# The value projection behind the output projection, and a feed-forward norm on transposed tokens

## The chip, the cores and the metric

The kernel runs on one core of a Trainium2 chip, in one launch. The metric is the time of the slowest core, here the only one, in microseconds of device time; lower is better. The engines are TensorE (PE, matmuls; PEld are its weight loads), VectorE (DVE), ScalarE (ACT), GpSimd (POOL) and SyncE (SP, which only issues transfers). Each has its own instruction queue and runs it in order. They wait for each other through semaphores.

## What is computed

The input is one sequence of 2048 tokens of 128 channels. A time-mixing layer comes first, then six layers of windowed attention and feed forward, then a layer norm. The change touches only the six layers (and takes one constant out of the first part). Cut to what matters:

```
for i in range(6):
    x = attn_layer(shift_tokens(x), Wqkv[i], ...) + x
    x = ffn_layer(shift_tokens(x), g[i], b[i], W1[i], b1[i], W2[i], b2[i]) + x

attn_layer:                              # 16 heads of 64, windows of 32 tokens
    q, k, v = split(x @ Wqkv)
    q, k = l2norm(q) * q_scale, l2norm(k) * k_scale
    q = q * cos * scale + rotate_half(q) * sin * scale      # and k, with 1 / scale
    out = softmax(8 * q @ k.T in the window and the one before) @ v
    return out @ Wo

ffn_layer:
    mu  = mean(x);  var = mean((x - mu) ** 2)               # over the 128 channels of a token
    xn  = (x - mu) / sqrt(var + 1e-5) * g + bln
    a, gate = split(xn @ W1 + b1)
    return a * gelu(gate) @ W2 + b2
```

`shift_tokens` takes the second half of the channels from the token before.

## The kernel before

The 2048 tokens are 16 tiles of 128, so the six layers are 96 tile steps, numbered s. The residual stream lies with channels on partitions, in `xa` (into attention) and `xb` (into feed forward). The work is a software pipeline, written out by hand: in step s the engines project tile p = s + 1 (q, k and v, and the norm and rotation of q and k), score tile a = s and weigh and sum tile b = s - 1. The feed forward works on two tiles at a time. In an odd step it makes the norm of a pair (`norm`) and narrows the pair before (`down`); in an even step it scales and widens (`up`). So two steps, an odd and an even one, are one period, and 48 such pairs make up the layers. A loop of 44 rounds holds most of them; the first and last steps are written out.

What sets the order is the source text alone: each engine has a `step` function, and its instructions go into that engine's queue as they stand there. No scheduler moves anything.

The banks in PSUM are shared. `bank_a` (`proj_a`) holds q, then v. `bank_b` (`proj_b`) holds k, then the narrowed product (second half, read into `xa`) and the norm's sums (first half), then two of the three widened chunks. `bank_s` (`att`) holds transposed probabilities, PV, the transposed heads and WO's product; `bank_t` (`turn`) the transposed q and k and the scores.

The lines that the steps below touch, with names as the profile gives them:
- TensorE: L1247 all transposes, L1280 projection of q, L1295 of k, L1306 PV, L1340 scores, L1352 projection of v, L1359 narrowing, L1364 centring (`centre` = identity less 1/128), L1371 spreading the deviations (`ones` times a diagonal), L1377 WO, L1383 variance, L1264 widening.
- VectorE: L1151 `sums` of squares, L88 to L104 an inverse root, L1176 `unit` (q, then k, divided by its norm), L1165 and L1168 `row_max` and `logits`, L1214 `norm_n`, L1219 `xa`, L1223 `xb`, L1228 `var_f`, L1234 `along` of k, L1183 `mass`.
- GpSimd: L1017 `turns`, L1025 and L1026 `shift_f`, L988 and L989 `shift_a`, L999 `across` of q, then of k, L1032 `along` of q, L1006 `rotated` of q, then of k, L1040 `rstd_f`.
- ScalarE: L1054 `squares`, L1083 and L1089 `q_t` and `k_t`, L1098 `rstd_diag`, L1104 `o_t`, L1113 the copy of v (`val`), L1061 `probs` (Exp), L1121 `normed`, L1128 and L1130 `dev` and `dev_sq`, L1068 gelu.
- SP: L945 and L948 spread a tile's v into windows, 16 transfers a step, once the copy of v is there.

Three waits matter around the change. The projection of q writes `bank_a`, so it waits for the copy of v (`v_laid`). The projection of k in an even step writes `bank_b`, so it waits for `var_kept` and for `xa_ready`, which VectorE raises when `xa` is done. And turning k waits for GpSimd's second `rotated`:

```python
pe.wait_ge(k_in, (layer_of(p) + 1) * 16)
after(pe, united[1], p)
if odd:
    after(pe, gated, NC_ * (h + 1))
else:
    if live["up"]:
        pe.wait_ge(var_kept, h + 2)
    after(pe, xa_ready, XA_BASE + h + 1 if not isinstance(h, int) or h >= 0 else 0)
```

Of the kernel before, what the change touches and what calls it, by code (L numbers as in the profile page):

```python
# [26 lines left out]
ALU = mybir.AluOpType  # L27
# [98 lines left out]
def build(nc, x, vectors, mix_w1, mix_w2, decay_w1, decay_w2, r_weights, r_norm, wqkv, wo, ffn, qk_scales,  # L126
          positions, carry, ident, band, level_masks, out):
    with ExitStack() as ctx:
# [15 lines left out]
        averager = sb("averager", [128, 128])  # L144
# [49 lines left out]
def time_mix(nc, ctx, given):  # L194
# [4 lines left out]
    xa, xb, x_tok, identity, identity_bf, band_f, band_bf, averager, ones, minus_half = (  # L199
        given[k] for k in ("xa", "xb", "x_tok", "identity", "identity_bf", "band_f", "band_bf", "averager",  # L200
# [14 lines left out]
    with ExitStack() as own:  # L215
# [105 lines left out]
        with nc.Block() as block:  # L321
# [26 lines left out]
            def _(pool):  # L348
                pool.memset(w2_wide[:, :, :], 0.0).then_inc(zeroed, 1)
                pool.memset(averager[:, :], 1.0 / DIM).then_inc(constants_made, 1)  # L350
# [4 lines left out]
                pool.wait_ge(constants_made, 3)  # L355
# [461 lines left out]
def layers(nc, ctx, given):  # L817
# [7 lines left out]
    xa, xb, identity, identity_bf, band_bf, averager, ones, minus_half = (  # L825
        given[k] for k in ("xa", "xb", "identity", "identity_bf", "band_bf", "averager", "ones", "minus_half"))
# [3 lines left out]
    with ExitStack() as own:  # L830
# [3 lines left out]
        def sem(name):  # L834
# [3 lines left out]
        centre = sb("centre", [128, 128])  # L838
# [25 lines left out]
        dev = sb("dev", [128, TWO])  # L864
        dev_sq = sb("dev_sq", [128, TWO])
        var_f = sb("var_f", [128, 2])
        rstd_f = sb("rstd_f", [128, 2])
        rstd_diag = sb("rstd_diag", [128, 2, TILE])
        norm_n = sb("norm_n", [128, TWO])
# [6 lines left out]
        cleared, centre_made = sem("cleared"), sem("centre_made")  # L876
# [17 lines left out]
        f_shifted, dev_made, deviated, dev_squared = (  # L894
            sem(k) for k in ("f_shifted", "dev_made", "deviated", "dev_squared"))
        var_made, var_kept, rstd_made, rstd_laid, rstd_spread, scaled_f, normed_f = (
            sem(k) for k in ("var_made", "var_kept", "rstd_made", "rstd_laid", "rstd_spread", "scaled_f", "normed_f"))
# [32 lines left out]
        with nc.Block() as block:  # L930
# [50 lines left out]
            def _(pool):  # L981
# [29 lines left out]
                def step(s, h, odd, live):  # L1011
# [8 lines left out]
                    if live["norm"]:  # L1020
                        pool.wait_ge(xb_ready, s - 1)
                        after(pool, dev_made, h + 1)
                        after(pool, rotated_in[1], p if live["p"] else STEPS)
                        after(pool, rstd_made, h + 1)
# [527 lines left out]
```

## Time and profile before

| what | us |
|---|---|
| median of three runs | 1976.1 (1976.05 to 1981.0) |
| the profiled execution | 1980.0 |
| its span, first to last instruction | 1978.2 |
| TensorE busy in it | 1822.9 (92%) |
| VectorE, GpSimd, ScalarE busy | 1550.4, 1455.8, 1168.9 |

A row of the order of time gives the start in us from the span's start, the length in us, the engine, the line, the operation, what it writes and reads, its shape and how many instructions the row joins; in brackets, how long the engine stood idle before it, and who ended that. A row that joins several instructions runs from the first one's start to the last one's end. An instruction may start a little before the row ahead of it ends, since the engines overlap the tail of one with the head of the next; so the cost of a piece of work on a busy engine is read from its start to the start of what follows. A float32 matmul appears as two instructions, a transpose as one. Between about 250 us and 1900 us the pairs of steps repeat with the same times, so one pair stands for all.

### The profile page before, as it was taken

The numbers are of one execution on the slowest core, as the hardware profiler recorded it, in microseconds if no ns is written. First come the engines' busy times: TensorE is split into PE (matmuls) and PEld (weight loads), VectorE is DVE, ScalarE is ACT, GpSimd is POOL, SyncE is SP. The second block draws the span as 40 slices with busy tenths as digits, with TensorE's granted clock in tenths as the row PEclk, the third lists the DMA queues.
The fourth block names the chain that finished last, engine by engine and source line by source line (L and its number), as shares of the span: only waits on it lengthen the run. The fifth ranks groups of instructions, "written<-read, shape, count | busy, mean of one in ns | idle before, by whom it ended". The sixth has DMA issues, their size and how long they took to land. (4 is left out here: it accounts for less than half of the span.)

```text
span 1978.2 us, 85596 instructions
## 1 busy us (share of the span) xinstructions
PE 1822.9 (92%) x34280; PEld 1307.5 (66%) x34280; DVE 1550.4 (78%) x2776; ACT 1168.9 (59%) x1966; POOL 1455.8 (74%) x967
## 2 busy tenths in 40 slices
PE   7874689999999999999999999999999999999995
PEld 3453366767776777776776767676767776777774
DVE  4665688888888888888888888888888888888874
ACT  2311356666666666666666666666666666666662
POOL 3131588888887888878878888788788887887871
PEclk9786799999999999999999999999999999999997
DMA  4000122223222223232223222223222232322220
GB/s 153 2 3 1 44 67 61 55 58 95 69 67 56 64 61 86 65 75 62 56 54 93 71 70 56 59 65 95 64 62 64 60 87 66 75 62 54 55 63 22
DMA packets 93582, 123.43 MB, mean 62 GB/s; under 512 B 27761, under 2 KB 41809, under 8 KB 93393
## 3 DMA queue, kind: packets, MB, share of 16 engines
q1 hardware_dynamic: 93232, 122.42, 24.6%
q8 instruction: 46, 0.75, 0.2%
q10 hardware_dynamic: 288, 0.13, 0.0%
q14 instruction: 16, 0.12, 0.0%
HBM read 20.74 MB, written 1.05 MB: 11 GB/s over the span
## 5 line engine op out<-in xcount | busy, mean ns | idle before, releaser
L999 POOL TENSOR_TENSOR across<-unit,turns 128x1024 f32<-128x1024 f32 x192 | 497.4, 2591 | 248.5 <-issue 236.9
L1006 POOL TENSOR_TENSOR rotated<-along,across 128x1024 f32<-128x1024 f32 x192 | 497.5, 2591 | 14.2
L1151 DVE TENSOR_REDUCE sums<-squares 128x16 f32<-128x1024 f32 x192 | 234.2, 1220 | 173.5 <-ACT squares L1054 173.4
L1247 PE MATMUL turn<-identity,rotated 128*128 128x128 f32 x1536 | 213.6, 282 | 32.1 <-ACT q_t L1083 21.6
L1032 POOL TENSOR_TENSOR along<-unit,turns 128x1024 f32<-128x1024 f32 x96 | 228.1, 2376 | 0.0
L1247 PEld LDWEIGHTS turn<-identity,rotated 128*128 128x128 f32 x1536 | 163.3, 141 | 68.9 <-ACT q_t L1083 43.2
L1352 PE MATMUL proj_a<-w_qkv,shift_a 128*128 128x512 f32 x384 | 190.4, 619 | 13.9 <-issue 5.8
L1306 PEld LDWEIGHTS att<-v_win,p_t 64*32 64x32 f32 x12288 | 142.0, 105 | 79.0 <-issue 73.6
L1377 PEld LDWEIGHTS att<-o_t,w_o 128*128 128x128 f32 x1536 | 187.9, 193 | 6.1 <-issue 1.0
L1377 PE MATMUL att<-o_t,w_o 128*128 128x128 f32 x1536 | 188.2, 276 | 0.0
L1280 PE MATMUL proj_a<-w_qkv,shift_a 128*128 128x512 f32 x384 | 183.8, 601 | 4.3 <-POOL shift_a L988 3.0
L1113 ACT COPY val<-proj_a 128x1024 f32<-128x1024 f32 x96 | 97.2, 1012 | 150.6 <-PE proj_a L1352 142.6
L1295 PE MATMUL proj_b<-w_qkv,shift_a 128*128 128x512 f32 x384 | 181.1, 594 | 0.0
L1083 ACT COPY q_t<-turn 128x512 f32<-128x512 f32 x192 | 103.2, 589 | 114.5 <-PE turn L1247 114.5
L1234 DVE TENSOR_TENSOR along<-unit,turns 128x1024 f32<-128x1024 f32 x96 | 166.4, 1733 | 0.0
L1054 ACT ACTIVATE squares<-proj_a 128x1024 f32<-128x1024 f32 x96 | 98.2, 1023 | 114.5 <-PE proj_a L1280 114.5
L1306 PE MATMUL att<-v_win,p_t 64*32 64x64 f32 x12288 | 162.9, 225 | 1.9 <-DMA v_win<-val 1.1
L1074 ACT COPY p_t<-att 128x512 f32<-128x512 f32 x192 | 103.2, 589 | 89.6 <-PE att L1247 89.6
L1340 PEld LDWEIGHTS turn<-k_t,q_t 64*32 64x32 f32 x12288 | 128.0, 105 | 41.7 <-issue 41.6
L1340 PE MATMUL turn<-k_t,q_t 64*32 64x64 f32 x12288 | 143.8, 226 | 0.3 <-issue 0.3
L1168 DVE TENSOR_TENSOR logits<-turn,row_max 128x512 f32<-128x512 f32 x192 | 132.7, 691 | 6.6
L1054 ACT ACTIVATE squares<-proj_b 128x1024 f32<-128x1024 f32 x96 | 98.3, 1024 | 63.8 <-PE proj_b L1295 63.8
(203 smaller groups left out, 3467.7 us busy)
## 6 DMA issues: line engine op xcount, KB each, us to landing
v_win<-val SPq DMA_DIRECT2D x1536, 64.0 KB
w_qkv<-wqkv_dram SPq DMA_DIRECT2D x18, 512.0 KB, 3.8
w_o<-wo_dram SPq DMA_DIRECT2D x6, 512.0 KB, 4.7
where<-positions_dram SPq DMA_DIRECT2D x1, 2048.0 KB, 10.6
w_ffn<-ffn_dram SPq DMA_DIRECT2D x12, 170.5 KB, 2.3
w_ffn<-ffn_dram SPq DMA_DIRECT2D x6, 192.0 KB, 2.3
x_tok<-x_dram SPq DMA_DIRECT2D x4, 256.0 KB, 4.2
out_dram<-final SPq DMA_DIRECT2D x4, 256.0 KB, 2.4
```

The costliest lines, as they stand in the source:

```text
L999: pool.tensor_tensor(a[:, :, ::-1, :], u, table, ALU.mult).then_inc(acrossed[j], 1)
L1006: pool.tensor_tensor(rotated[j][:, :, :], along[j][:, :, :], across[j][:, :, :], ALU.add).then_inc(rotated_in[j], 1)
L1032: pool.tensor_tensor(along[0][:, :, :], unit[0][:, :, :], turns[mine][:, 0, :].unsqueeze(1).broadcast_to([128, HEADS, HEAD]), ALU.mult).th ...
L1054: act.activation(squares[j][:, :, :], by_head((bank_a, bank_b)[j]), ACT.Square)\
L1151: dve.tensor_reduce(sums[:, j, :], squares[j][:, :, :], AX.X, ALU.add).then_inc(summed[j], 1)
L1247: mm = pe.transpose(bank[:, TILE * (i % 4):TILE * (i % 4) + TILE], buffer[:, TILE * i:TILE * i + TILE], identity[:, :])
L1280: mm = pe.matmul(bank_a[:, half, :], shift_a[mine][:, :], w_qkv[:, 512 * half:512 * half + 512], start=True, stop=True)
L1295: mm = pe.matmul(bank_b[:, half, :], shift_a[mine][:, :], w_qkv[:, base:base + 512], start=True, stop=True)
L1306: mm = pe.matmul(bank_s[WINDOW * w:WINDOW * w + WINDOW, par, HEAD * a_:HEAD * a_ + HEAD], p_t[rows, a_, WINDOW * w:WINDOW * w + WINDOW], v ...
L1340: mm = pe.matmul(bank_t[WINDOW * w:WINDOW * w + WINDOW, par, HEAD * a_:HEAD * a_ + HEAD], q_t[rows, a_, WINDOW * w:WINDOW * w + WINDOW], k ...
L1352: pe.matmul(bank_a[:, par, :].rearrange("p (a e) -> p a e", a=PAIRS), shift_a[mine][:, :], values[:, par, :, :], start=True, stop=True).th ...
L1377: mm = pe.matmul(bank_s[:, 0, 0:TILE], w_o[:, a_, :], o_t[:, a_, :], start=(a_ == 0), stop=(a_ == PAIRS - 1))
```

## The change

Two things are changed, both in `layers`.

First, in TensorE's order the projection of v goes behind WO: scores, WO, (norm's transposes), v, narrowing in an odd step; scores, (norm's transposes), WO, v, widening in an even one. ScalarE's copy of v moves accordingly, behind the second half of the exponentials. On VectorE `xa` moves from ahead of `xb` to the end of the step, behind `along`.

Second, the norm of the feed forward is computed with tokens on partitions. TensorE transposes the shifted input of the two tiles, ScalarE copies it out (`f_tok`), VectorE takes mean and variance with bn_stats and bn_aggr (the moments lie in `bank_b`) and makes `var_f` and `minus_mean`, GpSimd makes `rstd_f` (now behind the second `rotated`) and the new `offset_f` = minus_mean * rstd_f, ScalarE scales (`norm_tok`), TensorE transposes back, and ScalarE applies gain and bias straight from PSUM. The matmuls with `centre`, with the diagonal and with `averager` go, as do `dev`, `dev_sq`, `rstd_diag` and `norm_n`. The projection of k in an even step still waits for `var_kept` (now counted twice a pair) and for `xa_ready`.

The core of the diff:

```diff
 POOL
-                    if live["norm"]:
-                        pool.wait_ge(var_kept, h + 2)
-                        after(pool, rstd_laid, 2 * (h + 1))
-                        pool.tensor_tensor(rstd_f[:, :], var_f[:, :], minus_half[:, 0:2], ALU.pow).then_inc(rstd_made, 1)
                     if live["p"]:
                         add_turned(1, p)
+                    if live["norm"]:
+                        pool.wait_ge(var_kept, 2 * (h + 2))
+                        after(pool, scaled_f, 2 * (h + 1))
+                        pool.tensor_tensor(rstd_f[:, :], var_f[:, :], minus_half[:, 0:2], ALU.pow).then_inc(rstd_made, 1)
+                        pool.wait_ge(rstd_made, h + 2)
+                        pool.tensor_tensor(offset_f[:, :], minus_mean[:, :], rstd_f[:, :], ALU.mult).then_inc(offset_made, 1)
 ACT
-                        act.wait_ge(rstd_made, h + 2)
-                        after(act, rstd_spread, h + 1)
+                        act.wait_ge(offset_made, h + 2)
+                        after(act, norm_turned, h + 1)
                         for j in range(2):
-                            act.activation(rstd_diag[:, j, :], identity[:, :], ACT.Copy, scale=rstd_f[:, j:j + 1])\
-                                .then_inc(rstd_laid, 1)
+                            act.activation(norm_tok[:, j, :], f_tok[:, j, :], ACT.Identity, bias=offset_f[:, j:j + 1],
+                                           scale=rstd_f[:, j:j + 1]).then_inc(scaled_f, 1)
...
+                    if live["a"]:
+                        weigh(0)
+                    if live["up"]:
+                        act.wait_ge(norm_turned, h + 2)
+                        act.wait_ge(up_in, (layer_of(s - 4) + 1) * 48)
+                        after(act, widened, NC_ * (h + 1))
+                        act.activation(normed[:, :], bank_s[:, 1, 0:TWO], ACT.Identity, bias=w_ffn[:, F_B:F_B + 1],
+                                       scale=w_ffn[:, F_G:F_G + 1]).then_inc(normed_f, 1)
+                    if live["norm"]:
+                        act.wait_ge(f_turned, h + 2)
+                        after(act, scaled_f, 2 * (h + 1))
+                        act.copy(f_tok[:, :, :], bank_b[:, 0, 0:TWO].rearrange("p (j c) -> p j c", j=2)).then_inc(f_kept, 1)
+                    if live["a"]:
+                        weigh(1)
                     if live["p"]:
                         act.wait_ge(v_projected, 2 * p + 2)
...
 DVE
                     if live["a"]:
                         centre_scores(0)
-                    if live["up"]:
-                        dve.wait_ge(rstd_spread, h + 2)
-                        after(dve, normed_f, h + 1)
-                        dve.tensor_tensor(norm_n[:, :], dev[:, :], bank_s[:, 1, 0:TWO], ALU.mult).then_inc(scaled_f, 1)
-                    if live["a"]:
                         centre_scores(1)
-                    if live["down"]:
-                        ... (xa, moved behind along)
...
                     if live["norm"]:
-                        dve.wait_ge(var_made, h + 2)
-                        after(dve, rstd_made, h + 1)
-                        dve.tensor_scalar(var_f[:, :], bank_b[:, 0, TWO:TWO + 2], LN_EPS, None, ALU.add)\
-                            .then_inc(var_kept, 1)
+                        dve.wait_ge(f_kept, h + 2)
+                        for j in range(2):
+                            dve.bn_stats(f_stat[:, j, :], f_tok[:, j, :]).then_inc(f_stated, 1)
+                        dve.wait_ge(f_stated, 2 * (h + 2))
+                        stand_alone(dve, passed)
+                        moment = bank_b[:, 0, TWO:TWO + 4].rearrange("p (j m) -> p j m", j=2)
+                        for j in range(2):
+                            dve.bn_aggr(moment[:, j, :], f_stat[:, j, :]).then_inc(f_averaged, 1)
+                        dve.wait_ge(f_averaged, 2 * (h + 2))
+                        after(dve, offset_made, h + 1)
+                        dve.tensor_scalar(var_f[:, :], moment[:, :, 1], LN_EPS, None, ALU.add).then_inc(var_kept, 1)
+                        dve.tensor_scalar(minus_mean[:, :], moment[:, :, 0], -1.0, None, ALU.mult).then_inc(var_kept, 1)
...
 PE (behind the scores)
+                    if live["up"]:
+                        pe.wait_ge(scaled_f, 2 * (h + 2))
+                        if live["b"]:
+                            pe.wait_ge(o_laid, 2 * b + 2)
+                            stand_alone(pe, passed)
+                        for j in range(2):
+                            mm = pe.transpose(bank_s[:, 1, TILE * j:TILE * j + TILE], norm_tok[:, j, :], identity[:, :])
+                        mm.then_inc(norm_turned, 1)
+                    if live["b"]:
+                        ... (WO, moved here)
+                    if odd and live["p"]:
+                        pe.wait_ge(united[1], p + 1)
+                        stand_alone(pe, passed)
+                    if live["norm"]:
+                        if live["down"] and not live["p"]:
+                            pe.wait_ge(gated, NC_ * (h + 1))
+                        pe.wait_ge(f_shifted, 2 * (h + 2))
+                        for j in range(2):
+                            mm = pe.transpose(bank_b[:, 0, TILE * j:TILE * j + TILE], shift_f[:, TILE * j:TILE * j + TILE],
+                                              identity[:, :])
+                        mm.then_inc(f_turned, 1)
                     if live["p"]:
                         ... (the projection of v)
-                    if live["norm"]:
-                        pe.wait_ge(f_shifted, 2 * (h + 2))
-                        pe.matmul(bank_b[:, 0, 0:TWO], centre[:, :], shift_f[:, :], start=True, stop=True)\
-                            .then_inc(dev_made, 1)
-                    if live["up"]:
-                        pe.wait_ge(rstd_laid, 2 * (h + 2))
-                        ...
-                        pe.matmul(bank_s[:, 1, 0:TWO], ones[:, :], diag_flat, start=True, stop=True).then_inc(rstd_spread, 1)
-                    if live["norm"]:
-                        pe.wait_ge(dev_squared, h + 2)
-                        for j in range(2):
-                            mm = pe.matmul(bank_b[:, 0, TWO + j:TWO + j + 1], dev_sq[:, TILE * j:TILE * j + TILE],
-                                           averager[:, 0:1], start=True, stop=True)
-                        mm.then_inc(var_made, 1)
```

TensorE's queue in the last odd step written out ahead of the loop, from the scores to the next step's transposes, before (`w_o` is WO's weights, `averager` the variance's; the loop has the same, with register instructions between):

```order
L1340 MATMUL turn<-k_t,q_t 32x64 x64
L1352 MATMUL proj_a<-w_qkv,shift_a 128x512 x2
L1359 MATMUL proj_b<-hidden,w_ffn 128x256 x3
L1364 MATMUL proj_b<-shift_f,centre 128x256
L1377 MATMUL att<-o_t,w_o 128x128 x8
L1383 MATMUL proj_b<-averager,dev_sq 128x1 x2
L1247 MATMUL att<-identity,probs 128x128 x8
```

And in the changed kernel, whose lines are numbered a little differently (L1376 is the projection of v, L1356 WO):

```order
L1337 MATMUL turn<-k_t,q_t 32x64 x64
L1356 MATMUL att<-o_t,w_o 128x128 x8
L1367 MATMUL proj_b<-identity,shift_f 128x128 x2
L1376 MATMUL proj_a<-w_qkv,shift_a 128x512 x2
L1384 MATMUL proj_b<-hidden,w_ffn 128x256 x3
L1245 MATMUL att<-identity,probs 128x128 x8
```

WO has moved ahead of the projection of v, two transposes stand for the centring matmul, and nothing stands between narrowing and the next step's transposes.

VectorE's queue in the same odd step, from the second scores to the next step's `mass`, before:

```order
L1168 TENSOR_TENSOR logits<-turn,row_max 128x512
L1219 SCALAR_TENSOR_TENSOR xa<-proj_b,w_ffn,xb 128x256
L1223 TENSOR_TENSOR xb<-att,xa 128x128
L1228 TENSOR_SCALAR var_f<-proj_b 128x2
L1234 TENSOR_TENSOR along<-unit,turns 128x1024
L1183 TENSOR_REDUCE mass<-probs 128x16
```

And in the changed kernel:

```order
L1164 TENSOR_TENSOR logits<-turn,row_max 128x512
L1210 TENSOR_TENSOR xb<-att,xa 128x128
L1215 BN_STATS f_stat<-f_tok 128x6 x2
L1220 BN_AGGR proj_b<-f_stat 128x2 x2
L1223 TENSOR_SCALAR var_f<-proj_b 128x2
L1224 TENSOR_SCALAR minus_mean<-proj_b 128x2
L1229 TENSOR_TENSOR along<-unit,turns 128x1024
L1234 SCALAR_TENSOR_TENSOR xa<-proj_b,w_ffn,xb 128x256
L1179 TENSOR_REDUCE mass<-probs 128x16
```

`xa` has moved from the first place behind the logits to the last, and five small instructions stand ahead of `along`.

## Rows read from the trace of the kernel before

**Rows 1.** Busy us and count of each engine in a stretch, then TensorE's clock, DMA share.

```profile
900.00:1200.00 300.00, 291.49 (x5611) 212.24 (x5610) 248.68 (x439) 196.08 (x327) 244.89 (x161) 1.00 0.27 67
```

**Rows 2.** Order of time, TensorE, odd step and the even one's start: start, length, ...

```profile
1033.12 1.95 PE L1352 MATMUL proj_a<-w_qkv,shift_a 128*128 128x512 f32 x4 [0.18 <-DVE unit L1176]
1034.91 1.46 PE L1359 MATMUL proj_b<-hidden,w_ffn 128*128 128x256 f32 x6
1036.21 0.59 PE L1364 MATMUL proj_b<-shift_f,centre 128*128 128x256 f32 x2
1036.64 1.95 PE L1377 MATMUL att<-o_t,w_o 128*128 128x128 f32 x16
1038.42 0.50 PE L1383 MATMUL proj_b<-averager,dev_sq 128*128 128x1 f32 x4
1039.21 1.07 PE L1247 MATMUL att<-identity,probs 128*128 128x128 f32 x8 [0.28 <-issue]
1040.11 1.88 PE L1280 MATMUL proj_a<-w_qkv,shift_a 128*128 128x512 f32 x4
1041.83 1.88 PE L1295 MATMUL proj_b<-w_qkv,shift_a 128*128 128x512 f32 x4
...
1046.71 1.09 PE L1247 MATMUL turn<-identity,rotated 128*128 128x128 f32 x8 [0.31 <-ACT q_t L1083]
```

**Rows 3.** Order of time, TensorE, the even step before: WO and the widening.

```profile
1017.16 1.95 PE L1377 MATMUL att<-o_t,w_o 128*128 128x128 f32 x16
1019.08 1.99 PE L1264 MATMUL proj_b<-normed,w_ffn 128*128 128x256 f32 x8
```

**Rows 4.** Order of time, GpSimd, the odd step's rotation of q and k.

```profile
1033.15 2.36 POOL L999 TENSOR_TENSOR across<-unit,turns 128x1024 f32<-128x1024 f32 x1 [2.34 <-issue]
...
1037.92 2.35 POOL L1006 TENSOR_TENSOR rotated<-along,across 128x1024 f32<-128x1024 f32 x1
1040.23 3.34 POOL L999 TENSOR_TENSOR across<-unit,turns 128x1024 f32<-128x1024 f32 x1
1043.53 0.70 POOL L1040 TENSOR_TENSOR rstd_f<-var_f,minus_half 128x2 f32<-128x2 f32 x1
1044.21 2.37 POOL L1006 TENSOR_TENSOR rotated<-along,across 128x1024 f32<-128x1024 f32 x1
```

**Rows 5.** Order of time, VectorE, the odd step.

```profile
1031.79 1.23 DVE L1176 TENSOR_TENSOR unit<-proj_a,inv_norm 128x1024 f32<-128x1024 f32 x1
...
1036.10 0.69 DVE L1168 TENSOR_TENSOR logits<-turn,row_max 128x512 f32<-128x512 f32 x1
1036.71 0.47 DVE L1219 SCALAR_TENSOR_TENSOR xa<-proj_b,w_ffn,xb 128x256 f32 x1
1038.82 0.29 DVE L1223 TENSOR_TENSOR xb<-att,xa 128x128 f32 x1 [1.63 <-PE att L1377]
1039.02 0.15 DVE L1228 TENSOR_SCALAR var_f<-proj_b 128x2 f32<-128x2 f32 x1
1039.13 2.22 DVE L1234 TENSOR_TENSOR along<-unit,turns 128x1024 f32<-128x1024 f32 x1
1041.27 1.21 DVE L1183 TENSOR_REDUCE mass<-probs 128x16 f32<-128x1024 f32 x1
```

**Rows 6.** Order of time, VectorE and GpSimd in the even step before.

```profile
1019.54 1.22 DVE L1234 TENSOR_TENSOR along<-unit,turns 128x1024 f32<-128x1024 f32 x1
1019.71 3.27 POOL L1006 TENSOR_TENSOR rotated<-along,across 128x1024 f32<-128x1024 f32 x1
```

**Rows 7.** Order of time, VectorE, the last norm of the kernel.

```profile
1964.08 0.87 DVE L1441 BATCH_NORM_STATS2 stat<-total 128x6 f32<-128x128 f32 x4
1964.86 0.36 DVE L1444 BATCH_NORM_AGGREGATE moment<-stat 128x2 f32<-128x6 f32 x4
```

**Rows 8.** Order of time, ScalarE, the odd step: v's copy and the exponentials.

```profile
1035.18 1.01 ACT L1113 COPY val<-proj_a 128x1024 f32<-128x1024 f32 x1 [1.47 <-PE proj_a L1352]
1036.09 1.36 ACT L1061 ACTIVATE probs<-logits 128x512 f32<-128x512 f32 x2
```

More of the change, by code:

```diff
@@ L198, in time_mix @@
                            "ident", "band", "level_masks"))
-    xa, xb, x_tok, identity, identity_bf, band_f, band_bf, averager, ones, minus_half = (
-        given[k] for k in ("xa", "xb", "x_tok", "identity", "identity_bf", "band_f", "band_bf", "averager",
+    xa, xb, x_tok, identity, identity_bf, band_f, band_bf, ones, minus_half = (
+        given[k] for k in ("xa", "xb", "x_tok", "identity", "identity_bf", "band_f", "band_bf",
                            "ones", "minus_half"))
@@ L824, in layers @@
         given[k] for k in ("load_projection", "load_wo", "load_up", "load_down"))
-    xa, xb, identity, identity_bf, band_bf, averager, ones, minus_half = (
-        given[k] for k in ("xa", "xb", "identity", "identity_bf", "band_bf", "averager", "ones", "minus_half"))
+    xa, xb, identity, identity_bf, band_bf, ones, minus_half = (
+        given[k] for k in ("xa", "xb", "identity", "identity_bf", "band_bf", "ones", "minus_half"))
     bank_a, bank_b, bank_s, bank_t = (given[k] for k in ("proj_a", "proj_b", "att", "turn"))
@@ L837, in layers @@
         TWO = 2 * TILE
-        centre = sb("centre", [128, 128])
         magic = sb("magic", [128, 2, HEADS])
@@ L863, in layers @@
         shift_f = sb("shift_f", [128, TWO])
-        dev = sb("dev", [128, TWO])
-        dev_sq = sb("dev_sq", [128, TWO])
+        f_tok = sb("f_tok", [128, 2, TILE])
+        f_stat = sb("f_stat", [128, 2, 6])
         var_f = sb("var_f", [128, 2])
+        minus_mean = sb("minus_mean", [128, 2])
         rstd_f = sb("rstd_f", [128, 2])
-        rstd_diag = sb("rstd_diag", [128, 2, TILE])
-        norm_n = sb("norm_n", [128, TWO])
+        offset_f = sb("offset_f", [128, 2])
+        norm_tok = sb("norm_tok", [128, 2, TILE])
         normed = sb("normed", [128, TWO])
@@ L1345, in step @@
                                         mm.then_inc(scored, 1)
+                    if live["up"]:
[7 more added lines that the diff above has]
+                    if live["b"]:
+                        pe.wait_ge(wo_in, (layer_of(b) + 1) * 16)
+                        for a_ in range(PAIRS):
+                            if a_ % 4 == 0:
+                                pe.wait_ge(o_laid, 2 * b + a_ // 4 + 1)
+                            mm = pe.matmul(bank_s[:, 0, 0:TILE], w_o[:, a_, :], o_t[:, a_, :],
+                                           start=(a_ == 0), stop=(a_ == PAIRS - 1))
+                        mm.then_inc(attended, 1)
+                    if odd and live["p"]:
[9 more added lines that the diff above has]
+                        mm.then_inc(f_turned, 1)
                     if live["p"]:
@@ L1353, in step @@
                                       values[:, par, :, :], start=True, stop=True).then_inc(v_projected, 1)
+                    if not odd and live["p"]:
                         pe.wait_ge(united[1], p + 1)
```

62 lines of the change are left out of this document (15 added, 47 removed).

## The prediction

> **What bounds the kernel now.** I read the busy time of the engines in stretches first, then the order of time on each engine over one pair of steps. In the layers TensorE is busy 291.5 of 300 us at a granted clock of 1.00 [rows 1], and its rows follow each other with hardly a gap [rows 2]. So a pair of steps lasts as long as TensorE's list of work, as long as nobody makes it wait. The reader should therefore ask two things of every edit: does it shorten that list, and which wait stands ready to take the time back. All durations below are from one profiled execution of 1980.0 us; the runs' median is 1976.1, and I carry the difference over to that.
>
> Three waits stand close behind TensorE.
> - GpSimd's chain. From `unit` of q it runs two `across`, one `along`, two `rotated` and, in odd steps, `rstd_f` of 0.70 us [rows 4]. The last `rotated` ends at 1046.58 (1044.21 + 2.37), and TensorE starts to turn k at 1046.71 [rows 2, 4]: 0.13 us of slack.
> - The projection of k in even steps (L1295) writes the bank that `xa` (L1219) has to have read. Today `xa` is done at 1037.18 and the projection starts at 1041.83 [rows 2, 5]: 4.65 us of slack.
> - VectorE's `along` (L1234) and GpSimd's products do not run side by side. In the odd step `along` starts at 1039.13, inside `rotated` (1037.92 to 1040.27), and takes 2.22 us, 1.00 longer than its 1.22 in the even step; `across` behind it takes 3.34, not 2.36 [rows 4 to 6]. In the even step VectorE starts first (1019.54), keeps its 1.22, and `rotated` (from 1019.71) takes 3.27. So whoever starts first holds the other for the whole instruction.
>
> The Trainium skill, "SBUF — State Buffer", section "Who interferes with whom", says this outright: a VectorE instruction with two SBUF inputs contends with a GpSimd instruction that reads SBUF, and the later one is blocked to the end of the earlier one. These rows agree, with 2.22 against 1.22 us.
>
> **TensorE's list, part by part.** I count from one row's start to the next row's start.
> - Odd step, removed: the centring matmul, 0.43 us (1036.21 to 1036.64); the two variance matmuls with the wait for `xb` behind them, 0.79 (1038.42 to 1039.21, of which 0.28 is idle); and the 0.18 that V waits for `unit`, since V now stands 1.78 us later, behind WO. Together 1.40 [rows 2]. Added: two transposes of 128x128. Eight of them take 0.90 (1039.21 to 1040.11), so two cost 0.22. Net -1.18.
> - Even step, removed: the matmul that spreads the deviations, of the centring one's shape, 0.43; and the wait for `normed`, since WO to its successor takes 1.92 here (1017.16 to 1019.08) and 1.78 in the odd step, 0.14 [rows 2, 3]. Added 0.22. Net -0.35.
> - So TensorE's own list becomes 1.53 us shorter a pair. V moved behind WO is the same work; what it moves is the copy of V.
>
> **The copy of V.** ScalarE now makes it behind the second exponentials, and the next projection of q waits for it. The pair of exponentials ends at 1037.45, and the copy takes 1.01 [rows 8]: done by about 1038.5. TensorE would reach the projection of q at about 1038.9 (WO from 1032.94, then 1.78 + 0.22 + 1.79 + 1.30 for WO, transposes, V and the narrowing, and 0.90 for the transposes of the probabilities). Covered by 0.4 us, so nothing; without the cover it would be at most the copy's 1.01. In the even step the widening matmuls stand in between as well, so there is more cover; the gelu's table load now starts behind the copy, and its product has to be there by the odd projection of k. I put this at 0, with a bound of 0.35 (the whole gain of the even step). The spreading DMAs on SP's queue start behind this copy, some 2.2 us later, and are read two steps on: nothing.
>
> **GpSimd.** `rstd_f` leaves the place ahead of the last `rotated`: 0.70 off that chain. It and the new product `offset_f` come behind it. No row shows a product of two columns on GpSimd; it lies between 0 and the 0.70 of the power of two columns. I take 0.4, since a product is less work than a power. Either way the 2.34 us that GpSimd waits before its next `across` [rows 4] cover it. On ScalarE, two scalings of f_tok replace two of the identity, same shape and same place, and one copy replaces a copy and a square.
>
> **VectorE, where I think it is decided.** In the odd step the new order is second logits, `xb`, two bn_stats, two bn_aggr, `var_f`, `minus_mean`, `along`, and only then `xa`. The logits start at 1036.10 and the next instruction 0.61 later: `xb` at 1036.71 [rows 5]. WO has ended long before, so the 1.63 us that `xb` waits today goes. 0.20 later come the statistics: four bn_stats take 0.87 and four bn_aggr 0.36 in the last norm [rows 7], so 0.44 and 0.18 for two each; `var_f` and `minus_mean` 0.11 each (1039.02 to 1039.13); and some 0.05 to 0.1 for each of three waits on a result just made. That is 1036.91 + 0.44 + 0.18 + 0.22 + 0.25 = 1038.00 for `along`. GpSimd's `rotated` starts at 1037.92. GpSimd is ahead by 0.08 us, so `along` stands until 1040.27 and ends at 1041.35, just as today, although it was ready 1.1 us sooner. `xa` follows at 1041.27, as `mass` does today, takes 0.47, and is done at 1041.74. The projection of k starts 0.10 later, as V does behind `unit` (1033.02 to 1033.12): 1041.84, against 1041.83 today [rows 2, 5]. Queued behind it on TensorE are PV and all that follows.
>
> So the whole 1.18 us of the odd step turn into a wait at that projection, and a pair gains only the even step's 0.35, less 0.01: 0.34 us. Of the 48 pairs some 46 run in the steady state: -15.6 us. The last pairs lie open; removing about 1 us of norm there makes it -16 against 1980.0 on the profiled side, and **1961 us** against the median (rounded up by 1 for what else the wait may cost).
>
> **The rivals.**
> - B, VectorE is first. If the statistics take 0.1 us less than I worked out, `along` starts before `rotated`, as in the even step. `xa` is then done by about 1039.5, and the projection of k waits for nobody. `rotated` is pushed back 1.0 us, but `across` behind it no longer is. Next in line is GpSimd's chain, shorter by 0.70: with the even step's 0.35 a pair gains 1.05 (TensorE alone would give 1.53, but then it waits for `rotated`). 46 x 1.05 = 48 us: 1928. For it: the margin is 0.08 us in a sum of seven terms. Against: every wait term that I could have left out makes VectorE later.
> - C, slower: the statistics are themselves held by GpSimd. Then `along` is ready only after 1040.2, `across` has begun, and `along` waits for its end (1040.23 + 2.36 = 1042.59). `along` would end near 1043.7, `xa` near 1044.1, and the projection of k start at 1044.2, 2.36 late; less 0.35 that is +2.0 us a pair, +92 us: 2068. It decides from the point at which the chain is 2.2 us longer than I have it. Against: `mass`, which reads one SBUF operand, runs its 1.21 us through GpSimd's `across` [rows 4, 5], and bn_stats also reads one. The skill's section named above has the same: one SBUF input outside the two-port modes does not contend.
> - D, no change: what the even step gains is lost again, for instance by the gelu coming later behind the copy of V, so that the odd projection of k waits. -0.1 to 0 a pair: 1972 to 1976.
>
> **How the numbers follow.** Forecast (A) 0.57, B 0.20, D 0.11, C 0.12. A's own range is 1954 to 1968: 0.2 to 0.5 us a pair, from a wait of 0.15 more at the projection to 0.15 less. The range that should hold 8 in 10 takes in A, B and the lower half of D: 1924 to 1974; C and the rest of D are left out. A measurement of this kernel tells 0.3% (5.9 us) from no change. Faster by more than that are A and B, 0.77; within it D, 0.11; slower C, 0.12.
>
> **What would show it.** In the profile of the changed kernel: (1) the matmuls with `centre`, with the diagonal and with `averager` are gone, and transposes of 0.11 us stand there. (2) `along` of VectorE in odd steps still takes about 2.2 us or more, and lies across the end of GpSimd's `rotated`; if it takes 1.22 and `rotated` takes 3.3, it is B. (3) TensorE waits about 1.1 us before the projection of k in even steps, released by `xa`, some 46 times; in B it waits for `rotated` before turning k. (4) V no longer waits for `unit`, and the projection of q doesn't wait for the copy of V. (5) bn_stats take about 0.28 each; if they are longer than 1 us, it is C. TensorE's busy time falls by some 55 us in each case (0.59 + 0.59 + 0.50 less four eighths of 1.07, 48 times [rows 2]), so that number alone proves nothing. Wrong altogether would be a new wait that I have not named, above all at WO for `o_t`, behind ScalarE's scaling that waits for `offset_f`.

## The result, and the profile after

The changed kernel takes 1983.45 us (median of 20 runs, 1979.97 to 1991.94), the kernel before 1977.52 on the same chip (20 runs): a ratio of 1.0034, 95% interval 1.0025 to 1.0044. It is slower by a third of a per cent; 1961 was forecast, with 1924 to 1974 as the range. The profiled execution took 1985.96 us, its span 1984.2.

TensorE's busy time fell, VectorE's rose from 1550.4. The page's line of busy times, and from its costliest groups the projection of k (columns: count, busy us, mean ns, then the idle time before it and its releaser):

```profile
PE 1784.9 (90%) x34088; PEld 1254.1 (63%) x34088; DVE 1670.5 (84%) x2967; ACT 1153.4 (58%) x1918; POOL 1468.6 (74%) x1014
...
L1292 PE MATMUL proj_b<-w_qkv,shift_a 128*128 128x512 f32 x384 | 184.9, 604 | 59.8 <-DVE xa L1234 59.8
```

The second line is the wait that the prediction named: 59.8 us of TensorE before the projection of k, released by `xa`. So work left TensorE and came back as a wait. The rows of one even step show it, and a smaller one (order of time, TensorE, changed kernel; L1292 projects k, L1349 is the transposes of the norm, L1356 WO, L1376 the projection of v, L1261 the widening):

```profile
1011.52 1.95 PE L1292 MATMUL proj_b<-w_qkv,shift_a 128*128 128x512 f32 x4 [1.34 <-DVE xa L1234]
...
1020.43 0.44 PE L1349 MATMUL att<-identity,norm_tok 128*128 128x128 f32 x2
1020.70 1.95 PE L1356 MATMUL att<-o_t,w_o 128*128 128x128 f32 x16
1022.49 1.88 PE L1376 MATMUL proj_a<-w_qkv,shift_a 128*128 128x512 f32 x4
1024.48 1.99 PE L1261 MATMUL proj_b<-normed,w_ffn 128*128 128x256 f32 x8
```

From V to the widening it takes 1.99 us where V itself needs 1.72, as the projection of q does [rows 2]: TensorE waits 0.27 for `normed` (on the mean of the pairs 0.23), for which it waited 0.14 before the change, behind WO [rows 3]. ScalarE ends `normed` at 1024.43, and the widening starts 0.05 later:

```profile
1023.88 0.55 ACT L1115 ACTIVATE normed<-att,w_ffn 128x256 f32<-128x256 f32 x1
```

VectorE in the odd step ahead of that wait, the answer to [rows 5]:

```profile
1001.43 1.22 DVE L1172 TENSOR_TENSOR unit<-proj_a,inv_norm 128x1024 f32<-128x1024 f32 x1
...
1006.35 0.28 DVE L1210 TENSOR_TENSOR xb<-att,xa 128x128 f32 x1
1006.54 0.48 DVE L1215 BATCH_NORM_STATS2 f_stat<-f_tok 128x6 f32<-128x128 f32 x2
1007.16 0.26 DVE L1220 BATCH_NORM_AGGREGATE proj_b<-f_stat 128x2 f32<-128x6 f32 x2
1007.55 0.16 DVE L1223 TENSOR_SCALAR var_f<-proj_b 128x2 f32<-128x2 f32 x1
1007.63 0.15 DVE L1224 TENSOR_SCALAR minus_mean<-proj_b 128x2 f32<-128x2 f32 x1
1007.73 3.25 DVE L1229 TENSOR_TENSOR along<-unit,turns 128x1024 f32<-128x1024 f32 x1
1010.90 0.47 DVE L1234 SCALAR_TENSOR_TENSOR xa<-proj_b,w_ffn,xb 128x256 f32 x1
```

`along` is ready 0.19 us after GpSimd's `rotated` has begun (1007.54, next fence), stands until that ends and takes 3.25 us instead of 1.22. `xa` comes behind it and is done 9.94 us after `unit` began.

GpSimd in the same stretch, the answer to [rows 4]:

```profile
1007.54 2.35 POOL L1004 TENSOR_TENSOR rotated<-along,across 128x1024 f32<-128x1024 f32 x1
1009.86 3.33 POOL L997 TENSOR_TENSOR across<-unit,turns 128x1024 f32<-128x1024 f32 x1
1013.32 2.37 POOL L1004 TENSOR_TENSOR rotated<-along,across 128x1024 f32<-128x1024 f32 x1
1015.64 0.71 POOL L1039 TENSOR_TENSOR rstd_f<-var_f,minus_half 128x2 f32<-128x2 f32 x1
1016.43 0.20 POOL L1041 TENSOR_TENSOR offset_f<-minus_mean,rstd_f 128x2 f32<-128x2 f32 x1
1016.76 0.73 POOL L1015 TENSOR_TENSOR turns<-where,scales 128x256 f32 x1
1017.79 0.28 POOL L986 COPY shift_a<-xa 64x128 f32 x1 [0.30 <-POOL turns L1015]
1018.13 0.29 POOL L987 COPY shift_a<-xa 64x128 f32 x1
```

`rstd_f` and `offset_f` stand behind the last `rotated`, and the table product `turns` behind them, 15.33 us after `unit` (before: 14.7 on the mean). `rstd_f` stood ahead of the table before as well [rows 4], so what is new ahead of the table, and pushes it back by 0.6 us, is `offset_f` and the waits on results just made. That is what the prediction took for free. What runs beside it on VectorE is the inverse root: nine small instructions (L88 to L104) between `sums` and `unit`, each with two SBUF operands and 0.18 or 0.19 us when nothing is in its way. Its first rows, even step, changed kernel:

```profile
1016.90 0.63 DVE L88 SCALAR_TENSOR_TENSOR sums_min<-sums 128x32 f32<-128x32 f32 x1
1017.57 0.19 DVE L90 SCALAR_TENSOR_TENSOR inv_norm<-sums_min,magic 128x32 int32<-128x32 int32 x1
1017.79 0.33 DVE L92 TENSOR_TENSOR root_work<-inv_norm 128x32 f32<-128x32 f32 x1
1018.15 0.31 DVE L94 TENSOR_TENSOR root_work<-root_work,sums_min 128x32 f32<-128x32 f32 x1
```

The 0.63 us end with `turns`; 0.33 and 0.31 lie on the two shift copies. In the kernel before, the same step had

```profile
1011.35 0.18 DVE L88 SCALAR_TENSOR_TENSOR sums_min<-sums 128x32 f32<-128x32 f32 x1
1011.56 0.19 DVE L90 SCALAR_TENSOR_TENSOR inv_norm<-sums_min,magic 128x32 int32<-128x32 int32 x1
1011.79 0.30 DVE L92 TENSOR_TENSOR root_work<-inv_norm 128x32 f32<-128x32 f32 x1
```

beside

```profile
1010.72 0.73 POOL L1017 TENSOR_TENSOR turns<-where,scales 128x256 f32 x1
1011.76 0.28 POOL L988 COPY shift_a<-xa 64x128 f32 x1 [0.30 <-POOL turns L1017]
```

There the table is nearly done when the root begins. The Trainium skill, "SBUF — State Buffer", section "Who interferes with whom", has the rule (two SBUF inputs on VectorE, a GpSimd instruction that reads SBUF, the later one waits to the end). These rows agree: the price for an instruction of 0.19 us was up to 0.44 us.

In the odd step nothing was added on GpSimd, and yet the root is held there too, by the copies behind the table (GpSimd, then VectorE, changed kernel):

```profile
998.80 0.39 POOL L1022 COPY shift_f<-xb 64x256 f32 x1 [0.44 <-POOL turns L1015]
999.25 0.40 POOL L1023 COPY shift_f<-xb 64x256 f32 x1
```

```profile
998.96 0.28 DVE L88 SCALAR_TENSOR_TENSOR sums_min<-sums 128x32 f32<-128x32 f32 x1
999.28 0.42 DVE L90 SCALAR_TENSOR_TENSOR inv_norm<-sums_min,magic 128x32 int32<-128x32 int32 x1
```

To see the whole run, I took from the order of time, in every pair of steps, the start of the projection of k, of `unit` of q, and of the next projection of k, and the sum of the root's nine durations. Means over 42 to 44 pairs, us; a pair is the sum of the four distances (names as in the experiments below):

| kernel | odd: k to unit (root) | odd unit to next k | even: k to unit (root) | even unit to next k | pair |
|---|---|---|---|---|---|
| before | 7.43 (1.80) | 10.04 | 7.56 (1.94) | 10.78 | 35.81 |
| changed | 7.77 (2.15) | 10.10 | 8.04 (2.32) | 10.17 | 36.08 |
| xa first | 7.68 (2.05) | 8.64 | 8.36 (2.30) | 10.33 | 35.01 |
| small table | 7.54 (1.92) | 10.10 | 7.60 (1.88) | 10.29 | 35.53 |
| table late | 7.51 (1.89) | 10.10 | 7.49 (1.79) | 10.34 | 35.44 |
| late, even steps | 7.58 (1.95) | 10.10 | 7.50 (1.79) | 10.34 | 35.52 |
| late, odd steps | 7.56 (1.94) | 10.10 | 7.97 (2.24) | 10.17 | 35.80 |
| xa first, table late | 7.33 (1.71) | 8.89 | 7.63 (1.82) | 10.81 | 34.66 |
| before, product | 7.43 (1.81) | 10.04 | 7.93 (2.31) | 10.76 | 36.16 |
| before, small table | 7.57 (1.94) | 10.04 | 7.49 (1.86) | 10.86 | 35.96 |
| before, table late | 7.41 (1.71) | 10.07 | 7.34 (1.71) | 12.23 | 37.05 |
| before, xa last | 7.43 (1.80) | 10.10 | 7.51 (1.81) | 10.79 | 35.83 |
| before, V behind WO | 7.57 (1.95) | 10.25 | 7.48 (1.85) | 10.54 | 35.84 |
| changed, V ahead | 7.42 (1.79) | 10.10 | 8.04 (2.34) | 10.77 | 36.33 |

The change took 0.61 us from one column (even unit to k), and added 0.34 and 0.48 to the two that hold the root, and 0.06 where `xa` waits: +0.27 a pair. The root's own time explains 0.73 of the 0.82 added ahead of `unit`.

The 0.61 is not all saved work. 0.48 of it is the even step's `unit` coming later, for which TensorE no longer waits there, since V stands behind WO; from k to k the even step became only 0.13 shorter. The late `unit` is paid in two other places: at `normed`, and in the odd step. GpSimd's chain starts at that `unit`, so its next table starts 4.0 us behind the odd step's k instead of 3.4, and the copies behind it fall onto the odd step's root.

From the first `unit` to the last it is 1709.1 us, before 1699.0 (the rows of `unit`, below: durations, then first and last start); the last pairs and the final norm behind them took 63.7 us instead of 69.4, the start 1.6 more, and so the span grew by 6.0.

```profile
L1172 DVE TENSOR_TENSOR unit<-proj_a,inv_norm x96: 1223/1224/1226, 211.4 to 1920.5; 128x1024 f32<-128x1024 f32 x96
```

```profile
L1176 DVE TENSOR_TENSOR unit<-proj_a,inv_norm x96: 1223/1224/1225, 209.8 to 1908.8; 128x1024 f32<-128x1024 f32 x96
```

### The profile page after: what moved, and what is told of

Same layout as the page of the kernel before. It is cut to its first block and busy times, and to the rows that moved or that the text cites. A ratio compares the mean times of both kernels' runs of the same rounds, so it can differ in the third digit from the quotient of the medians.

```text
span 1984.2 us, 85402 instructions
## 1 busy us (share of the span) xinstructions
PE 1784.9 (90%) x34088; PEld 1254.1 (63%) x34088; DVE 1670.5 (84%) x2967; ACT 1153.4 (58%) x1918; POOL 1468.6 (74%) x1014
## 3 DMA queue, kind: packets, MB, share of 16 engines
HBM read 20.74 MB, written 1.05 MB: 11 GB/s over the span
## 5 line engine op out<-in xcount | busy, mean ns | idle before, releaser
L1060 ACT ACTIVATE probs<-logits 128x512 f32<-128x512 f32 x192 | 121.0, 630 | 233.0 <-DVE logits L1164 233.0
L1229 DVE TENSOR_TENSOR along<-unit,turns 128x1024 f32<-128x1024 f32 x96 | 250.9, 2613 | 0.0
L1292 PE MATMUL proj_b<-w_qkv,shift_a 128*128 128x512 f32 x384 | 184.9, 604 | 59.8 <-DVE xa L1234 59.8
L1356 PE MATMUL att<-o_t,w_o 128*128 128x128 f32 x1536 | 192.1, 278 | 0.0
L1376 PE MATMUL proj_a<-w_qkv,shift_a 128*128 128x512 f32 x384 | 183.1, 599 | 7.4 <-DVE unit L1172 7.4
L1277 PE MATMUL proj_a<-w_qkv,shift_a 128*128 128x512 f32 x384 | 184.7, 604 | 3.2 <-POOL shift_a L987 1.9
L1356 PEld LDWEIGHTS att<-o_t,w_o 128*128 128x128 f32 x1536 | 178.9, 192 | 5.3
L1292 PEld LDWEIGHTS proj_b<-w_qkv,shift_a 128*128 128x128 f32 x384 | 69.9, 191 | 167.9 <-issue 165.1
```

Source lines behind the costliest of these rows:

```text
L1229: dve.tensor_tensor(along[1][:, :, :], unit[1][:, :, :], turns[mine][:, 2, :].unsqueeze(1).broadcast_to([128, HEADS, HEAD]), ALU.mult).the ...
L1277: mm = pe.matmul(bank_a[:, half, :], shift_a[mine][:, :], w_qkv[:, 512 * half:512 * half + 512], start=True, stop=True)
L1292: mm = pe.matmul(bank_b[:, half, :], shift_a[mine][:, :], w_qkv[:, base:base + 512], start=True, stop=True)
L1356: mm = pe.matmul(bank_s[:, 0, 0:TILE], w_o[:, a_, :], o_t[:, a_, :], start=(a_ == 0), stop=(a_ == PAIRS - 1))
```

## The experiments

Theory 1: the gain is eaten where `xa` stands behind `along`. Theory 2: it is eaten by the root, which GpSimd's table product and copies hold. Both can hold at once. The prediction had theory 1's wait in its sum already, so the time above its forecast has to come from something else. Ratios are to the kernel before, run on the same chip in turn; the changed kernel's is 1.0034.

**xa ahead of along**, in the changed kernel:

```
+ if live["down"]: dve.wait_ge(narrowed, h + 1); dve.scalar_tensor_tensor(xa[...]) ...
  if live["p"]: ... dve.tensor_tensor(along[1] ...)
- if live["down"]: dve.wait_ge(narrowed, h + 1); dve.scalar_tensor_tensor(xa[...]) ...
```

> The changed kernel with xa put ahead of along, behind minus_mean; nothing else. Theory 1 (xa behind along is what eats the gain): TensorE's wait of 1.34 us before the projection of k in even steps goes, and a pair of steps gets 0.8 to 1.3 us shorter, so 1983 - 46 x 0.8 to 1.3 = 1923 to 1946. Theory 2 (GpSimd's table product and shift copies hold VectorE's inverse root, because GpSimd's chain starts at unit and the root starts behind k): the wait goes as well, but the root of the even step then starts 1.1 to 1.3 us earlier against the same GpSimd instructions, is held longer, and unit comes hardly sooner: 0 to 0.3 us a pair, 1969 to 1983, with the root's nine instructions in even steps above their 2.32 us of now.

Measured: 1936.04 us, ratio 0.9800 (0.9783 to 0.9818). TensorE in the even step:

```profile
1017.93 1.88 PE L1292 MATMUL proj_b<-w_qkv,shift_a 128*128 128x512 f32 x4
...
1021.29 1.09 PE L1245 MATMUL turn<-identity,rotated 128*128 128x128 f32 x8
1023.78 1.09 PE L1245 MATMUL turn<-identity,rotated 128*128 128x128 f32 x8 [1.40 <-POOL rotated L1004]
```

The wait for `xa` is gone, worth 47 us, as theory 1 has it. Theory 2's forecast for this kernel was wrong: the root does stay at 2.30 us and k to `unit` grows to 8.36 (the root starts 0.3 later behind k), but that gives back only 0.32 of 1.46. The next bound is GpSimd's last `rotated`, as rival B had said.

**A product more behind the last rotated**, in the kernel before:

```
  add_turned(1, p)
+ pool.wait_ge(rotated_in[1], ...)
+ pool.tensor_tensor(spare[:, :], minus_half[:, 0:2], minus_half[:, 2:4], ALU.mult).then_inc(spared, 1)
+ pool.wait_ge(spared, h + 2)
```

> The kernel before with one more product of two columns on GpSimd behind the last rotated of odd steps, with a wait on a result just made, as offset_f has it; its result is used by nobody. Theory 2: the table product of the even step comes 0.4 to 0.5 us later, falls onto the root, which goes from 1.94 to about 2.3 us, and since V waits for unit the pair gets 0.2 to 0.4 us longer: 1985 to 1995. Theory 1: 0.2 us of GpSimd in front of a time in which it waits for unit costs nothing: 1975 to 1978.

Measured: 1994.60 us, ratio 1.0091 (1.0076 to 1.0106). GpSimd, then VectorE, in an even step:

```profile
1018.32 0.20 POOL L1047 TENSOR_TENSOR spare<-minus_half 128x2 f32<-128x2 f32 x1
1018.82 0.75 POOL L1019 TENSOR_TENSOR turns<-where,scales 128x256 f32 x1 [0.31 <-POOL spare L1047]
```

```profile
1019.01 0.61 DVE L90 SCALAR_TENSOR_TENSOR inv_norm<-sums_min,magic 128x32 int32<-128x32 int32 x1
...
1020.24 0.31 DVE L96 SCALAR_TENSOR_TENSOR root_work<-root_work 128x32 f32<-128x32 f32 x1
```

An instruction of 0.20 us that nobody reads, ahead of a wait of 2.34 us, costs 18 us: with its waits it moves the table 0.63 later (table's start after k: 4.70 to 5.33), the root goes from 1.94 to 2.31. This is the price of a product like `offset_f`, measured by itself in the kernel before, where V still waits for `unit`; theory 1 has no place for it.

**The table cut to one column**, first in the changed kernel, then in the kernel before:

```
- pool.tensor_tensor(turns[mine][:, :, :], where[:, tile_of(p), :, :], scales[:, layer_of(p), :, :], ALU.mult)
+ pool.tensor_tensor(turns[mine][:, 0, 0:1], where[:, tile_of(p), 0, 0:1], scales[:, layer_of(p), 0, 0:1], ALU.mult)
```

> The changed kernel with the table product `turns` cut to one column of 128 (the rotation tables stay at a constant, so the rotation isn't computed; all waits stay). Theory 2: GpSimd is done 0.5 to 0.6 us sooner in every step, the root's nine instructions fall from 2.15 and 2.32 us back to 1.7 to 1.9, unit comes 0.3 to 0.45 us sooner in each step: 0.6 to 0.9 a pair, 1942 to 1955. Theory 1: the table does not lie between unit of the odd step and xa, the wait of 1.34 stays and so does the pair but for 0 to 0.2 us: 1974 to 1983.

> The same cut of the table product in the kernel before. There the root takes 1.80 and 1.94 us, against 1.72 with nobody in its way. Theory 2: at most 0.3 us a pair to win, of which TensorE's own list leaves 0 to 0.2: 1966 to 1976, so clearly less than the same cut wins in the changed kernel. If it wins as much here (0.6 to 0.9 a pair, 1935 to 1948), the table is a cost of both kernels and no answer to why the change lost.

Both kernels fill the tables once with a constant, and so leave out the rotation.

Measured: 1959.48 us, 0.9909 (0.9896 to 0.9922) in the changed kernel, and 1982.90, 1.0037 (1.0024 to 1.0051) in the one before. The direction is theory 2's, the first size a little under it, and the second missed: less work on GpSimd made the kernel before slower. In odd steps the copies behind the table now come sooner and fall onto the root (GpSimd, then VectorE):

```profile
1031.74 0.29 POOL L991 COPY shift_a<-xa 64x128 f32 x1 [0.38 <-POOL shift_f L1029]
1032.10 0.29 POOL L992 COPY shift_a<-xa 64x128 f32 x1
```

```profile
1031.78 0.30 DVE L88 SCALAR_TENSOR_TENSOR sums_min<-sums 128x32 f32<-128x32 f32 x1
1032.11 0.32 DVE L90 SCALAR_TENSOR_TENSOR inv_norm<-sums_min,magic 128x32 int32<-128x32 int32 x1
```

So it is the moment that counts, not the amount.

**The table behind the root**, same work, in the changed kernel: behind the shift copies, with a wait.

```
  shift_input(...)
+ pool.wait_ge(rooted, ROOT_OPS * p + ROOT_OPS)
+ ... turns[mine] = where * scales (moved from the step's beginning)
  cross(0, p, mine)
```

Two waits that the new order needs come with it (for the last `rotated`, and for `offset_f`). The shift copies, no longer behind the table, come sooner by it, so the run moves them too.

> The changed kernel with GpSimd's table product moved behind its shift copies and made to wait for the last of the root's nine instructions, so that it runs beside unit, which reads PSUM and one SBUF operand; same work. Theory 2 (the root is held by what GpSimd does at that moment): the root falls from 2.15 and 2.32 us to about 1.9 in both steps, unit comes 0.2 to 0.4 us sooner in each: 0.4 to 0.8 us a pair, 1946 to 1965, while TensorE's wait for xa stays at 1.3 us or more. Rival: the table, now in front of GpSimd's first product, delays its chain by as much as it frees: 1980 to 1990.

Measured: 1953.19 us, 0.9889 (0.9870 to 0.9909), inside the range of theory 2. The pair is 0.37 us shorter than before the change: with the two roots at 3.68 us together, as before the change (3.74), the forecast's 0.34 appears, with the wait for `xa` still in it (10.10 us).

**The same in one kind of step alone:**

```
- if live["p"]: ... turns[mine] = where * scales
+ if odd and live["p"]: ... turns[mine] = where * scales
  ...
+ if not odd and live["p"]: pool.wait_ge(rooted, ...) ... turns[mine] = where * scales
```

This is the form with the late table in even steps; the other has `odd` and `not odd` exchanged.

> The changed kernel with the late table product in even steps alone, the steps in which rstd_f and offset_f had pushed it back. Theory 2: the even step's root falls from 2.32 to about 1.8 us and its unit comes 0.4 to 0.55 us sooner, the odd step stays at 2.1 to 2.2: 0.3 to 0.5 us a pair, 1958 to 1970.

> The same in odd steps alone, in which nothing was added on GpSimd, and the root met the table only because k is projected sooner after unit of the even step. Theory 2: the odd step's root falls from 2.15 to about 1.9, the even step's stays at 2.3: 0.15 to 0.35 us a pair, 1966 to 1977. If the odd step's loss has another cause, 1980 to 1985.

Measured: even steps 1955.99 us, 0.9901 (0.9879 to 0.9922), a little better than expected; odd steps 1969.30, 0.9953 (0.9936 to 0.9970). The two gains, 27 and 14 us against 1983.45, are more than the 30 of both: with the even step mended alone the odd step's root also falls, from 2.15 to 1.95, since the distance from `unit` to k changes by 0.17 and with it where the copies meet the root. The even step, with `offset_f` ahead of its table, is the larger part. In this run TensorE no longer waits for `normed` either: from V to the widening it takes 1.72 us on the mean, for 1.95 in the changed kernel.

**The late table in the kernel before**, the same edit of both kinds of step:

```
- ... turns[mine] = where * scales
  shift_input(...)
+ pool.wait_ge(rooted, ROOT_OPS * p + ROOT_OPS)
+ ... turns[mine] = where * scales
```

> The late table product in both steps, in the kernel before. The root there takes 1.80 and 1.94 us against 1.7 with nobody in its way, so there is at most 0.3 us a pair to win, and TensorE's list bounds both steps: 0 to 0.3 us a pair, 1962 to 1977, against 0.65 in the changed kernel. If it wins 0.6 here too, the collision was there before and the change didn't bring it.

Measured: 2029.08 us, ratio 1.0253 (1.0230 to 1.0277). The expectation was wrong by over 50 us, though the root did fall to 1.71 in both steps, free of any wait. VectorE, GpSimd and TensorE in the even step:

```profile
1002.21 3.38 DVE L1236 TENSOR_TENSOR along<-unit,turns 128x1024 f32<-128x1024 f32 x1
```

```profile
1002.16 2.35 POOL L1006 TENSOR_TENSOR rotated<-along,across 128x1024 f32<-128x1024 f32 x1
```

```profile
1008.49 1.95 PE L1297 MATMUL proj_b<-w_qkv,shift_a 128*128 128x512 f32 x4 [1.29 <-DVE hidden L1194]
```

Before, VectorE was first there by 0.17 us [rows 6]. Now GpSimd is first by 0.05: `along` takes 3.38 us instead of 1.22, `hidden` behind it is late, and TensorE waits 1.29 us for it. A collision of 0.3 us was removed and one of 2.2 put in its place.

**xa behind along alone**, in the kernel before:

```
- if live["down"]: ... xa[...]
  if live["b"]: ... xb[...]
  if live["norm"]: ... var_f
  if live["p"]: ... along[1]
+ if live["down"]: ... xa[...]
```

> The kernel before with nothing but xa moved behind along. By the prediction's arithmetic xa is then done at 1041.74 and the projection of k starts 0.10 later, 0.01 us behind its time of now: 0 to 0.1 us a pair slower, 1975 to 1982, with a wait for xa that is about nothing; so xa behind along costs only what the projection of k would otherwise have won.

Measured: 1977.15 us, 0.9993 (0.9977 to 1.0009): nothing, as expected. The odd `unit` to k goes from 10.04 to 10.10.

**The parts apart: V behind WO with the old norm, and the new norm with V in its old place.** The order on TensorE in the first, and then in the second (names for groups of instructions):

```
- scores, V, narrowing, centring, spreading, WO, variance, widening
+ scores, spreading, WO, centring, V, narrowing, variance, widening
```

```
- scores, norm back, WO, norm in, V, narrowing, widening
+ scores, V, narrowing, norm in, norm back, WO, widening
```

The copy of V on ScalarE moves with it; in the first, the copy and square of the deviations stand ahead of the second exponentials.

> The kernel before with the projection of v (and ScalarE's copy of it) behind the output projection, the norm as it was. The waits of V for unit (0.18 us) and of xb for the output projection (1.63 us) go. TensorE's list is the bound from unit of the odd step to the next projection of k: 0 to 0.3 us a pair gained, 1962 to 1976. Rival (the late copy of V or the late normed costs): 0.2 us a pair or more lost, above 1985.

> The changed kernel with the projection of v and its copy at their old place ahead of the output projection, the new norm kept. xb then waits for the output projection again and the statistics come later, along and xa with them, and GpSimd's later table product is still there: 0.1 to 0.5 us a pair slower than the changed kernel, 1986 to 2006. Rival (moving V is what lost the time): faster than the changed kernel, 1955 to 1976.

Measured: 1975.13 us, 0.9978 (0.9954 to 1.0003), and 1996.43, 1.0091 (1.0077 to 1.0106). Moving V alone changes the time by less than the runs can tell. Two things cancel in it: from k to k the even step becomes 0.32 us shorter and the odd step 0.35 longer, above all by a wait ahead of the transposes of the probabilities (0.28 before [rows 2]):

```profile
1034.35 1.06 PE L1247 MATMUL att<-identity,probs 128*128 128x128 f32 x8 [0.75 <-issue]
```

VectorE's `xb`, which here still stands behind `xa` and so behind the later narrowing, ends 0.10 us before that row; that it is what TensorE waits for is read from the rows and not tested. The new norm by itself loses 19 us, nearly all of it ahead of the even step's `unit` (8.04 for 7.56), about the price of the bare product above. The even step's 0.61 is there in full only when both parts are (V alone 0.24, the norm alone 0.01).

**Both mended**, xa first and the table late, that is the edit of the first experiment and that of the late table in both steps:

> Both: xa ahead of along, and the table product behind the root. If the two losses are separate, their gains add up to what GpSimd's chain allows: TensorE already waits 1.40 us there for the last rotated, but a sooner unit starts that chain sooner: 1936 less 0.3 to 0.7 us a pair, 1904 to 1922. If GpSimd's chain is the whole bound by then, 1932 to 1938.

Measured: 1919.78 us, ratio 0.9709 (0.9693 to 0.9725), the fastest of all, 2.9% under the kernel before. 64 us against the changed kernel, where the two parts alone gave 47 and 30: the gains are separate for the most part. GpSimd's table now waits for the root and runs beside `unit`, and what is left of TensorE's wait there is on `rotated`:

```profile
1002.40 0.73 POOL L1028 TENSOR_TENSOR turns<-where,scales 128x256 f32 x1 [2.37 <-DVE inv_norm L104]
```

```profile
1016.33 1.09 PE L1249 MATMUL turn<-identity,rotated 128*128 128x128 f32 x8 [0.91 <-POOL rotated L1004]
```

## Why the prediction was wrong

- **TensorE's list.** Right in the odd step: 1.18 us were forecast; from WO to the next projection of k it takes 7.75 us once nothing waits (1010.18 to 1017.93, xa first) against 8.89 before from the same point, V then first (1032.94 to 1041.83): 1.14. TensorE's busy time fell by 38.0 us and not by 55: the rows of two transposes take 0.43 and 0.44 us (the first in the row below, the second in the even step above), where two eighths of 1.07 had been put for each, and 48 x (0.59 + 0.59 + 0.50 - 0.43 - 0.44) is 39.

```profile
1004.10 0.43 PE L1367 MATMUL proj_b<-identity,shift_f 128*128 128x128 f32 x2
```

- **along is held, and xa with it (forecast A).** Right. Ready at `unit` + 6.30 (forecast 6.21), against `rotated` at + 6.11 (6.13); `along` ended at + 9.55 (9.56), `xa` at + 9.94 (9.95), k started at + 10.09 (10.05, on the mean 10.10). The wait was 59.8 us in 45 pairs, 1.33 each, where 1.1 had been said. Taking it away alone gave 47 us, so it held most of the odd gain (46 x 1.18 is 54), and TensorE then waits for `rotated` instead.
- **The statistics.** 0.48 and 0.26 us for two each, forecast 0.44 and 0.18. Two bn_stats ran inside GpSimd's `along` without loss: rival C fell.
- **The copy of V, ScalarE.** Covered, as forecast; V behind WO alone costs nothing.
- **The step that failed: "Either way the 2.34 us that GpSimd waits before its next `across` [rows 4] cover it."** `offset_f` itself took 0.20 us, within its bounds. But the idle time lies behind the table product and the shift copies, and `offset_f` stands ahead of these: with its waits it moves them 0.6 us. I asked who waits for GpSimd, found nobody, and did not ask what VectorE does while GpSimd runs. The root does it: +0.38 in the even step, 0.48 ahead of `unit`. The bare product in the kernel before shows the same (+0.37), and with the table moved behind the root the time is 1953, under the forecast.
- **A second part of the same step, not priced at all:** GpSimd's chain starts at `unit`, so whatever shortens the way from `unit` to k brings the next root closer to that chain, a late `unit` too. The odd step's root lost 0.35 us with nothing added on GpSimd there; with the even step's table late it lost 0.15. With `xa` at a fixed 10.10 behind `unit`, a later `unit` in the odd step goes into the pair in full.
- **"The wait for `normed`, 0.14", was to go.** It did not: since `unit`, the logits and the exponential ahead of `normed` come later, TensorE waits 0.27 at the widening, and with the even step's table late it does not. From k to k the even step gained 0.13 and not 0.35, and the odd step, put at 0, lost 0.40.
- **The rivals.** D was the nearest (what the even step gains is lost again), but by the gelu; its mechanism was not this one. The slower rival was the wrong mechanism too. B's next bound holds: xa first frees `xa` by other means, and came out at 1936 with TensorE waiting for `rotated`, 0.80 us a pair under the kernel before, where 1928 and 1.05 stood.

## What to carry to other kernels

An engine's idle time hides added work only if nothing that stands between the work and the idle time collides with another engine: list what moves with it, and what the neighbour does at its new time. Where two engines hold each other up, ask who is first and by how much; a margin of 0.2 us decided over 2 us here, and making either side faster can lose. Before giving up an edit, look for the instruction that can stand elsewhere at no cost: here one move ahead of `along`, and one wait.

## What was not expected of the hardware

- Instructions of 0.19 us on VectorE took up to 0.63 us, in the rows above, beside a GpSimd product of 128x256, and 0.28 to 0.42 beside GpSimd copies of 64 partitions, which have a single SBUF operand.
- Less work was slower twice: a table product of 0.20 us instead of 0.73 cost 0.37%, and an undisturbed root (1.71 us for 1.80 and 1.94) 2.5%, both by who came first elsewhere.
